# ScalarE's and the transfer queue's rounds written out, with waits on constants, in a Mamba block with experts

## The reference

```python
xr = x @ W_in                                   # 128 -> 2 x 256
xi, res = jnp.split(xr, 2, axis=-1)
xc = causal_conv(xi, conv_w, 4 taps) + conv_b
u = silu(xc)
dbc = u @ W_x                                   # 256 -> 8 + 16 + 16
delta = softplus(dbc[..., :8] @ W_dt + b_dt)
deltaA = exp(delta[..., None] * -exp(A_log))    # 16 states per channel
h_t = deltaA_t * h_(t-1) + delta_t * B_t * u_t  # a scan over the 256 tokens
y = (sum over n of h[..., n] * C[..., n] + u * D) * silu(res)
x = x + y @ W_out
...
scores = x_flat @ gate_w.T;  top 2, softmax -> cw
for e in range(E):
    y = y + cw[:, e:e+1] * (silu(x_flat @ w1[e].T) @ w2[e].T)
x = x + y
```

## Time and profile before

| | us |
|---|---|
| median of 3 runs (1090.12 to 1092.07) | 1091.39 |
| the profiled execution | 1092.1 |
| its span, first to last instruction | 1090.0 |
| TensorE busy | 1040.8 (95%) |
| VectorE busy | 1017.5 (93%) |
| GpSimd busy | 959.6 (88%) |
| ScalarE busy | 907.1 (83%) |
| table loads of ScalarE ahead of hidden (L906) | 56 of 1.283 |

### The profile page before, as it was taken

One profiled execution on the slowest core, in us unless ns is written; L12 is line 12 of the kernel. 1 busy time (PEld: TensorE's weight loads), 2 busy tenths in 40 slices (PEclk: granted clock), 3 DMA queues, 4 the chain that ended last, 5 costly groups with the idle time before them and its releaser, 6 DMA issues.

```text
span 1090.0 us, 18707 instructions
## 1 busy us (share of the span) xinstructions
PE 1040.8 (95%) x6150; PEld 758.0 (70%) x6150; DVE 1017.5 (93%) x1057; ACT 907.1 (83%) x1379; POOL 959.6 (88%) x890
## 2 busy tenths in 40 slices
PE   7787789999999999999999999999999999989998
PEld 4445466677777777777776777777777776767776
DVE  5999999999999999999999999999999999999822
ACT  4987867988989999998989899899989989875533
POOL 4688886999999999999999999999999999799934
PEclk9698989999999999999999999999999999989999
DMA  5332111122040312204031311403130130320000
GB/s 202 137 127 77 71 48 79 59 108 78 1 158 28 127 59 103 82 9 173 3 126 58 126 58 40 145 0 126 58 136 39 66 109 0 137 87 11 11 8 14
DMA packets 37364, 84.12 MB, mean 77 GB/s; under 512 B 3320, under 2 KB 28208, under 8 KB 28976
## 3 DMA queue, kind: packets, MB, share of 16 engines
q1 hardware_dynamic: 36880, 83.06, 21.4%
q10 hardware_dynamic: 416, 0.30, 0.1%
HBM read 78.63 MB, written 4.72 MB: 76 GB/s over the span
## 4 chain that ended last, share of the span: by engine, by line
PE 83%; DVE 9%; issue 4%; ACT 3%; DMA 0%; POOL 0%; DVEq 0%; ACTq 0%; POOLq 0%
PE work L1829 19%; PE work L1806 18%; PE y_ps L1758 18%; PE work L1682 8%; DVE h L1258 6%; PE rows L1737 4%; PE work L1779 3%; PE work L1666 2%; PE work L1701 2%; PE rows L1829 2%; PE work L1692 2%; PE rows L1806 1%; DVE rows L1248 1%; PE y_ps L1747 1%; PE work L1727 1%
## 5 line engine op out<-in xcount | busy, mean ns | idle before, releaser
L551 POOL TENSOR_TENSOR h<-h,c_rows 128x1024 f32<-128x1024 f32 x256 | 599.9, 2364 | 53.5 <-DVE h L1258 53.2
L1258 DVE TENSOR_TENSOR_SCAN h<-dA,rows 128x1024 f32<-128x1024 f32 x256 | 579.0, 2276 | 1.1
L872 ACT ACTIVATE dA<-delta,a_neg 128x510 f32<-128x510 f32 x512 | 325.7, 707 | 7.9 <-DVE h L1258 4.4
L1248 DVE TENSOR_TENSOR rows<-du,rows 128x1024 f32<-128x1024 f32 x256 | 306.7, 1214 | 4.9 <-PE rows L1737 4.9
L1758 PEld LDWEIGHTS y_ps<-ident,h 128*128 128x128 f32 x2048 | 241.2, 144 | 62.3 <-issue 34.5
L1758 PE MATMUL y_ps<-ident,h 128*128 128x128 f32 x2048 | 270.0, 278 | 10.3 <-POOL h L551 10.3
L1829 PEld LDWEIGHTS work<-w,hid 128*128 128x128 f32 x1856 | 223.3, 193 | 34.5 <-ACT hid L906 18.9
L1806 PE MATMUL work<-x2T,w 128*128 128x512 f32 x474 | 240.2, 602 | 2.9 <-ACT u L790 2.3
L1829 PE MATMUL work<-w,hid 128*128 128x128 f32 x1856 | 229.1, 277 | 2.4 <-ACT hid L906 2.2
L906 ACT ACTIVATE hid<-work 128x512 f32<-128x512 f32 x237 | 139.3, 596 | 65.5 <-PE work L1806 63.7
L591 POOL TENSOR_TENSOR x<-x,weighted 128x512 f32<-128x512 f32 x127 | 161.9, 1274 | 19.6 <-DVE weighted L1340 19.2
(11 more groups left out here) (147 smaller groups left out, 941.7 us busy)
## 6 DMA issues: line engine op xcount, KB each, us to landing
c_rows<-c_dram SPq DMA_DIRECT2D x64, 1024.0 KB, 5.0
x_in<-in_x SPq DMA_DIRECT2D x16, 256.0 KB, 3.0
x_again<-in_x SPq DMA_DIRECT2D x16, 256.0 KB, 3.4
out<-x SPq DMA_DIRECT2D x15, 256.0 KB, 2.6
w<-in_w1T SPq DMA_DIRECT2D x1, 1024.0 KB, 4.8
w<-in_w2T SPq DMA_DIRECT2D x1, 1024.0 KB, 7.0
h<-in_conv_w SPq DMA_DIRECT2D x1, 512.0 KB, 4.9
c_dram<-bcd SPq DMA_DIRECT2D x16, 32.0 KB, 1.6
```

The lines of the kernel that those rows point to most:

```text
L551: nc.gpsimd.tensor_tensor(at, at, c_rows[:, n, :].unsqueeze(1).broadcast_to([P, H, T]), ALU.mult).then_inc(c_used, 1)
L872: last = nc.scalar.activation(two_seqs(dA[:, n % RING, half, :])[:, :, 1:], two_seqs(delta[:, half, :])[:, :, 1:], ACT.Exp, scale=a_neg[:, ...
L1248: nc.vector.tensor_tensor(rows[:, n % 2], du[:, j.odd], rows[:, n % 2, H - 1, :].unsqueeze(1).broadcast_to([P, H, T]), ALU.mult).then_inc( ...
L1258: nc.vector.tensor_tensor_scan(h[:, n % RING].rearrange("p h t -> p (h t)"), dA[:, n % RING].rearrange("p h t -> p (h t)"), rows[:, n % 2] ...
```

## The change

A function written_out is added that runs a body for each round with constant numbers. ScalarE's rounds 5 to 15 and the transfer queue's 7 to 18 go through it in place of run. TensorE, VectorE and GpSimd keep their loops. The steps, their order and what each waits for are as before; all lines from 119 on move down by five.

```diff
--- before.py
+++ after.py
@@ -115,6 +115,11 @@
             body(Round(loop_first, it))
             body(Round(loop_first + 1, it))
         for i in range(loop_first + 2 * pairs, stop):
+            body(Round(i))
+
+    def written_out(body, first, stop):
+
+        for i in range(first, stop):
             body(Round(i))
 
     with ExitStack() as ctx:
@@ -445,7 +450,7 @@
             load_c(r[3], 0)
             load_c(r[3], 1)
             load_x(r[6])
-            run(sp, round_, 7, 7, 19)
+            written_out(round_, 7, 19)
             load_again(r[14])
             load_c(r[15], 2)
             load_again(r[15])
@@ -1128,7 +1133,7 @@
             hidden(r[1], 1, 0)
             hidden(r[1], 1, 1)
             decay(r[3], 7)
-            run(act, round_, 5, 4, 16)
+            written_out(round_, 5, 16)
             decay(r[14], 8)
             decay(r[14], 9)
             hidden(r[12], 2, 0)
```

## The result

The changed kernel takes 1109.2 us (median of 4 runs, 1108.1 to 1110.9) against 1091.3 us before (median of 4 runs as well, one more than in the table above). The ratio is 1.0162, with a 95% interval of 1.0150 to 1.0174: 17.9 us slower, where 18.1 was forecast. Its profiled execution took 1109.0 us, its span 1107.0 us, which is 17.0 us more than before.

A forecast was written before the change was run, and what follows sets the result against it. TensorE was taken to bound the kernel, so ScalarE costs only where TensorE waits. Terms 8.7 + 5.5 + 3.4 + 0.6 = 18.2 us, taken as 18.1 on the 1091.4 us median, gave 1109.5 us, range 1105 to 1113.5.

The forecast's parts named there:

- A: At hidden(2,0): TensorE's step from hidden(2,1) to expert(1) grows by 0.87 us, ten times: 8.7 us.
- B: At hidden(3,0): TensorE's step from project_gate to delta_rank grows by 0.55 us, ten times: 5.5 us.
- The order of the waits: In ScalarE's hidden, 35 table loads of 1.28 us move from ahead of the wait for TensorE's product to behind it.
- The sum of the four places: Losses on TensorE at A, B, C and D of a round: 8.7 + 5.5 + 3.4 + 0.6 = 18.2 us.
- C: At hidden(5,0): TensorE's step from row_b(13) over hidden(6,0) to expert(5) grows by 0.34 us, ten times: 3.4 us.
- D: At hidden(0,0), loop's first body only, five rounds: between 0 and 1.3 us, taken as 0.6 us.
- second rival: Only A and D cost something, B and C's samples perhaps holding TensorE's own form: 9.3 us, 1100.7 us; chance 0.05.
- The second way, from the periods: Ten rounds at 64.66 us plus TensorE's loop turns, 646.6 to 648.5 against 629.50 us: 17.1 to 19.0 us more.
- The loop's turns: Four idle times of ScalarE where its loop turns, 1.8 us in all, vanish; worth 0 to 1.8 us, taken as 0.
- third rival: ScalarE's long straight code is fetched late in every round, 0.6 us, ten rounds 6 us: 1115.5 us; chance 0.06.
- The transfer queue: Its 12 written-out rounds cost nothing: it waits for ScalarE's copy of C, and GpSimd never waits for a transfer.
- The forecast for the page: Signs in the changed profile: idle time ahead of hidden's table loads from 22.5 to 45-50 us, periods 64.6 to 65.0 us.

The follow-up runs named there:

- e1: Changed kernel with hidden's two waits exchanged at 35 places (A, B, C of rounds 6 to 15, D of the even ones): 1.0005 against the kernel before.
- e2: Kernel before, loops kept, with hidden's two waits exchanged at the same 35 places in the loop's bodies: 1.0161 against the kernel before.
- e8: Changed kernel with TensorE's rounds 5 to 15 written out as well: 1.0161 against the kernel before.
- e6: Changed kernel with hidden's two waits exchanged at B alone, rounds 6 to 15: gives back 0.0033, 3.6 us, of the changed kernel's 1.0162.
- e7: Changed kernel with hidden's two waits exchanged at C alone, rounds 6 to 15: gives back 0.0028, 3.1 us, of the changed kernel's 1.0162.
- e3: Changed kernel with ScalarE's loop put back, only the transfer queue's rounds written out: 1.0001 against the kernel before.
- e5: Changed kernel with hidden's two waits exchanged at A alone, rounds 6 to 15: gives back 0.0068, 7.4 us, of the changed kernel's 1.0162.
- e9: Kernel before, loops kept, with hidden's two waits exchanged only in the rounds outside the loop: 0.9953 against the kernel before.
- e10: Changed kernel with hidden's two waits exchanged at all 56 places: 0.9946 against the kernel before.
- e11: Changed kernel with the table load asked for ahead of both waits of hidden: 0.9945 against the kernel before.

## Why the prediction was right

**The bound.** TensorE sets the round, and only what it waits for counts: shown by its waits, ten at A and ten at B, and by ScalarE's busy time, which hardly changed (907.1 and 906.1 us) while the kernel lost 1.6%.

**The order of the waits.** Right, and shown from both sides by e1 and e2. One part of the reading was wrong: expert_done had not been met long before at A. There the load in the loop waits 0.74 us, and what ends it is TensorE's expert, L1829. It changed nothing in the sum, which took A's step with that wait in it.

**The sum of the four places.** The terms against the changed kernel's own steps: A 10 x (1.94 - 1.10) = 8.4 us, put at 8.7. C 10 x (1.41 - 1.08) = 3.3 us, put at 3.4. D 5 x (0.53 - 0.43) = 0.5 us, put at 0.6 as the middle of 0 to 1.3, which was a guess that came out. B 10 x (1.32 - 0.86) = 4.6 us, put at 5.5: this is the term that was mis-sized, by 0.9 us, because its sample came from a round in which TensorE too was written out (e8). The prediction named that risk as its second rival, at the full 5.5 + 3.4 us; the true share was a tenth of that, and e6 and e7 give B and C back, so the rival itself is wrong. The four sum to 16.8 us. The ten rounds are 16.87 us longer; of what is not in the four, the first A of the ten is 0.3 us longer than the others, and the turns of TensorE's loop are 0.3 us shorter together.

**The second way, from the periods.** 17.1 to 19.0 us, against 16.87: a little too high, since the period of 64.66 us is that of a round with TensorE written out (e8), and the changed kernel's rounds are 64.52 us without a turn of TensorE's loop. With one they are 0.2 us longer, where the kernel before has 0.4 to 0.5.

**The median.** 1109.5 was given, 1109.2 was measured. The span grew by 17.0 us and the median by 17.9, since the profiled run of the kernel before was the slowest of its four. The terms came out at 16.9 where 18.1 was taken, so about 1 us of the agreement in the median is luck.

**The loop's turns.** Their 1.8 us of idle ScalarE were taken at 0. The four idle times ahead of L877 are gone from the changed kernel's waits, and e1 shows no gain that goes with them. As forecast. In the changed kernel the profile lists no idle time of ScalarE that nothing explains from 269 us on, so the third rival, late pieces of the long code, did not appear either.

**The transfer queue.** Taken at nothing; e3 measures 1.0001, and GpSimd waits for no transfer in the changed kernel.

**The forecast for the page.** Idle time ahead of the loads 45 to 50 us, measured 46.6; periods 64.6 to 65.0 us, measured 64.52 and 64.74, slightly under.

## What to carry to other kernels

When an engine's stream holds an instruction that depends on nothing (a table load here), look where it ends up between the waits in the built program: the same two lines of source gave one order with constants and the other at most places with registers, and unrolling exchanged them. A kernel that is partly looped and partly written out holds both forms, so the trace before the change already has a sample of what the change makes. Compare one round inside the loop with one outside, step by step on the engine that sets the pace; here that comparison alone gave the ten rounds' loss to within 1.3 us, and pointed to two lines whose exchange gains 5 us.

## What the runs showed of the hardware

The turn of TensorE's loop showed less time where TensorE had waited longer at A. The product ahead of the turn and the first one behind it, in the kernel before, in the changed one and in e5, where only A is exchanged:

```profile
427.18 0.38 PE L1717 MATMUL work<-parts,minus 96*96 96x512 bf16 x1
427.63 0.59 PE L1779 MATMUL work<-w_out,yT 128*128 128x128 f32 x3
```

```profile
431.63 0.38 PE L1722 MATMUL work<-parts,minus 96*96 96x512 bf16 x1
431.97 0.71 PE L1784 MATMUL work<-w_out,yT 128*128 128x128 f32 x4
```

```profile
429.01 0.38 PE L1726 MATMUL work<-parts,minus 96*96 96x512 bf16 x1
429.54 0.37 PE L1788 MATMUL work<-w_out,yT 128*128 128x128 f32 x1
```

The step over the turn is 0.45 us before, 0.34 us in the changed kernel and 0.53 us in e5, against 0.21 us where there is no turn (364.52 from 364.31 in the kernel before). Over the four turns of each trace it goes with the step at A, eight microseconds ahead: 0.31 to 0.36 us where A takes 1.94 or 1.95 us (changed, e6, e7), 0.39 to 0.58 where it takes 1.08 to 1.16 (before, e1, e3, e5, e9, e10), 0.56 to 0.62 where it takes 0.96 (e11). The spread within the middle group stays unexplained. So giving A back in e5 saved 8.6 us at its step and lost 0.8 us at the turns, which is why 7.8 us came. The likely reason, that the sequencer does part of the turn's work beside the wait, is not shown.

With its rounds written out, TensorE started about 0.09 us later behind ScalarE's hid than in its loop: 1.41 against 1.32 us at B, 2.04 against 1.94 us at A (e8 and the changed kernel). With all its rounds written out this cost as much as its loop's turns gave. That it is the wait on a constant, and not something else in the written-out form, is argued and not shown, and why it is slower stays open.
